# Starting the next chunk's ScalarE work before the current chunk's ladder on VectorE, in the input quantization of an adaLN block

## The chip, the cores and the metric

The kernel runs on one Trainium2 chip, on all 8 NeuronCores, each with one of the 8 batch elements. No data passes between the cores. The time is the device time in microseconds of the slowest core.

## What is computed

The reference is one adaLN layer on x of shape (8, 2048, 1024), with a gated recurrent mixer and a quantized feed-forward network. Cut to what matters here:

```python
def bitlinear(x, W, b):
    w_scale = clip(mean(abs(W)), EPS, None)
    Wq = clip(round(W / w_scale), -1, 1) * w_scale
    x_scale = clip(max(abs(x), axis=-1, keepdims=True), EPS, None)
    xq = clip(round(x * (127 / x_scale)), -128, 127) * (x_scale / 127)
    return einsum('bnd,hd->bnh', xq, Wq) + b

mod = silu(c) @ wmod            # six vectors: sa, ca, ga, sb, cb, gb
h = layernorm(x) * (1 + ca) + sa
x = x + ga * mixer(h)           # three 1024x1024 products, a scan over 2048 tokens
h = layernorm(x) * (1 + cb) + sb
x = x + gb * bitlinear(gelu(bitlinear(h, W1, b1)), W2, b2)   # hidden size 4096
```

The change touches the rounding of x in the first `bitlinear`: every element of h, times 127 over its token's maximum, is rounded to an integer.

## The kernel before, in words

A core holds its 2048 tokens along the free dimension and the 1024 features as KC = 8 chunks of 128 partitions. A chunk is a tile of 128x2048 in bf16. `X`, `Hh` and `X2` each hold eight chunks. The program is written engine by engine: `p.on(engine, function, wait, inc)` appends a function to the engine's list, with the semaphore counts that it waits for and the one that it increments. Order on an engine is the order of these calls. `sDV` counts VectorE's steps, `sAC` ScalarE's. Behind the functions stands the class `Ser` (line 85 on), which makes each VectorE, ScalarE and GpSimd instruction wait for the one before it on the same engine; nearly all rows therefore carry its line, L100 (the wait itself is L99). Where a function increments a counter, `ser_flush_wait` (L92) waits for the engine's last instruction first, and then the counter goes up; L56 is the increment behind it in `p.on`, L51 the one of a step without an instruction.

The stages in order: loads and statistics of the weights, the mixer (L734), the second layer norm with the scales of each token, the quantization of h, the first feed-forward product (L1066), the ternary form of W2, the second product (L1306, with the quantization of the hidden values in it), and its other three groups (L1346).

The quantization of h runs between `build_bcast`, which puts 127 over the token's maximum into `B127`, and `emit_tern`, which prepares the first weight slab. It goes over the eight chunks in `Hh`, in place. `xlad_u` multiplies the chunk by `B127` into `QUU` (VectorE). `xlad_act` takes the absolute value into `QY` and the sign into `QSG` (ScalarE). `xlad_dve` rounds on VectorE with a ladder: it adds 128, takes 127.5 off into `QRA`, and for the bits 64 down to 1 compares `QRA` with the bit into `QT` and subtracts; then it takes the integer part, puts the sign back and writes the chunk. `QUU`, `QAU`, `QY`, `QR0`, `QRA`, `QRB`, `QT`, `QNA` are eight 2048-wide parts of `X`, whose contents are no longer needed; `QSG` is `RB`. The names with R0, RB, NA and `QAU` are not used by the loop before; `MB` was the broadcast mean of the layer norm and is free by then. The first product waits for `xq_done`, the count after the last chunk.

The quantization of the hidden values in the second product (L1306's stage) has the same ladder on pairs of chunks of 128x4096, and there the multiply of the next pair is already placed inside the ladder of the current one (`emit_ulad`).

Of the kernel before, what the change touches and what calls it, by code (L numbers as in the profile page):

```python
# [8 lines left out]
AF = mybir.ActivationFunctionType  # L9
ALU = mybir.AluOpType  # L10
# [4 lines left out]
KC = D // 128  # L15
# [91 lines left out]
def build_nc():  # L107
    nc = bass.Bass("TRN2", target_bir_lowering=False)
    p = Prog()
# [43 lines left out]
    def sb(name, shape, dt):  # L153
        return nc.alloc_sbuf_tensor(name, shape, dt).ap()

    X = sb("X", [128, KC * L], BF16)
    Hh = sb("Hh", [128, KC * L], BF16)
# [3 lines left out]
    MB = sb("MB", [128, L], BF16)  # L161
# [5 lines left out]
    B127 = sb("B127", [128, L], BF16)  # L167
# [31 lines left out]
    QUU, QAU = XS(0, 2048), XS(2048, 4096)  # L199
    QY, QR0 = XS(4096, 6144), XS(6144, 8192)  # L200
    QRA, QRB = XS(8192, 10240), XS(10240, 12288)
    QT, QNA = XS(12288, 14336), XS(14336, 16384)
    QSG = RB[:, 0:2048]
# [43 lines left out]
    for s in semnames:  # L247
        p.sem(s)

    chunk = lambda t, k: t[:, k * L:(k + 1) * L]  # L250
# [4 lines left out]
         inc=("sCN", 16), dma=True)  # L255
    p.on("scalar", lambda E: E.dma_start(out=CPB[:], in_=cpack_b),
         inc=("sCN", 16), dma=True)
    p.on("scalar", lambda E: E.dma_start(out=IDNF[:], in_=idnf),
         inc=("sCN", 16), dma=True)
# [3 lines left out]
    for k in range(KC):  # L263
# [3 lines left out]
             wait=w, inc=(sx, 16))  # L267
        p.on("vector", lambda E, k=k: E.tensor_copy(chunk(X, k), xstg[k % 2]),
             wait=[(sx, p.cnt[sx])], inc=("sDV", 1))
# [3 lines left out]
         wait=[("sCN", cn_all)], inc=("sAC", 1))  # L273
# [143 lines left out]
    for t in range(48):  # L417
# [4 lines left out]
            inc=("sMD", 1) if t == 47 else None)  # L422
    mm_modc = p.cnt["sMD"]
    p.on("vector", lambda E: E.tensor_copy(MODC[:], PB[2][:, 0:48]),
         wait=[("sMD", mm_modc)], inc=("sDV", 1))
# [43 lines left out]
    def ws2_fin(E):  # L469
# [10 lines left out]
         wait=[("sDV", ws2_done)])  # L480
    p.on("tensor", lambda E: E.matmul(PB[7][:, 1:2], ONESRf[:],
                                      WSrow[0:1, 3:4], start=True, stop=True),
         inc=("sMM", 1))
# [11 lines left out]
    for k in range(KC):  # L495
        wv = [("sDV", modc_done)] if k == 0 else []
        for j in range(NNT):
# [3 lines left out]
                wait=wv if j == 0 else [],  # L501
                inc=("sM3", 1) if (k == KC - 1 and j == NNT - 1) else None)
# [17 lines left out]
    for k in range(KC):  # L520
        wv = [("sM3", st1_mm[k - 2])] if k >= 2 else []
        p.on("vector", lambda E, k=k: E.tensor_tensor(
            sq1[k % 2], chunk(X, k), chunk(X, k), ALU.mult),
            wait=wv, inc=("sDV", 1))
        sqdv = p.cnt["sDV"]
        for j in range(NNT):
# [4 lines left out]
                wait=[("sDV", sqdv)] if j == 0 else [],  # L531
                inc=("sM3", 1) if j == NNT - 1 else None)
# [28 lines left out]
    for j in range(NNT):  # L561
# [3 lines left out]
            wait=[("sAC", rstd1_ac)] if j == 0 else [],  # L565
            inc=("sM3", 1) if j == NNT - 1 else None)
# [10 lines left out]
    for j in range(NNT):  # L577
# [3 lines left out]
            wait=[("sAC", bc1e_ac)] if j == 0 else [],  # L581
            inc=("sM3", 1) if j == NNT - 1 else None)
# [12 lines left out]
    for k in range(KC):  # L595
        wv = [("sDV", bc1_done)] if k == 0 else [("sAC", p.cnt["sAC"])]

        def ln_apply_v(E, k=k, src=X):
# [6 lines left out]
            wait=[("sDV", p.cnt["sDV"])], inc=("sAC", 1))  # L605
# [79 lines left out]
    if DEBUG_TAPS:  # L685
        p.on("gpsimd", lambda E: E.dma_start(out=tap_hln, in_=Hh[:]),
             wait=[("sAC", p.cnt["sAC"])], inc=("sTAP", 16), dma=True)
        p.on("gpsimd", lambda E, v=p.cnt["sTAP"]: E.wait_ge(sems["sTAP"], v))
        p.on("gpsimd", lambda E: E.dma_start(out=tap_mod, in_=MODC[:]),
             inc=("sTAP", 16), dma=True)  # L690
# [179 lines left out]
    for k in range(KC):  # L870
        wv = [("sDV", bc2_done)] if k == 0 else []

        def h2_v(E, k=k):
# [6 lines left out]
            wait=[("sDV", p.cnt["sDV"])], inc=("sAC", 1))  # L880
        acn = p.cnt["sAC"]
        M1n = XS(4096, 6144)
        if k == 0:
# [3 lines left out]
                wait=[("sAC", acn)], inc=("sDV", 1))  # L887
        else:
# [3 lines left out]
                wait=[("sAC", acn)], inc=("sDV", 1))  # L892
# [4 lines left out]
        inc=("sDV", 1))  # L897
# [38 lines left out]
    def build_bcast(vec_tile, out_tile, after_dv):  # L936
        for g4 in range(4):
            pp = g4 % 2
            wv = [("sDV", after_dv)] if g4 == 0 else []
            if g4 >= 2:  # L940
                wv += [("sAC", p.cnt["sAC"])]
            for b4 in range(4):
                blk = g4 * 4 + b4
                p.on("vector", lambda E, blk=blk, b4=b4, v=vec_tile, pp=pp:
                     E.tensor_scalar(
                         WSB[:, (pp * 4 + b4) * 128:(pp * 4 + b4) * 128 + 128],
                         IDN[:], v[:, blk:blk + 1], None, ALU.mult),
                     wait=wv if b4 == 0 else [], inc=("sDV", 1))
                dvn = p.cnt["sDV"]
                p.on("tensor", lambda E, blk=blk, b4=b4, pp=pp: E.matmul(  # L950
                    PB[pp][:, b4 * 128:(b4 + 1) * 128], ONES128[:],
                    WSB[:, (pp * 4 + b4) * 128:(pp * 4 + b4) * 128 + 128],
                    start=True, stop=True),
                    wait=[("sDV", dvn)],
                    inc=("sMM", 1) if b4 == 3 else None)
            mmn = p.cnt["sMM"]
            p.on("scalar", lambda E, g4=g4, o=out_tile, pp=pp:
                 E.activation(o[:, g4 * 512:(g4 + 1) * 512],
                              PB[pp][:, 0:512], AF.Identity),
                 wait=[("sMM", mmn)], inc=("sAC", 1))  # L960
        p.on("vector", None, wait=[("sAC", p.cnt["sAC"])], inc=("sDV", 1))
        return p.cnt["sDV"]

    b127_done = build_bcast(VB127, B127, xs_done)
    bs1_done = build_bcast(VBS1, BS1, b127_done)

    def xlad_u(E, src_bf):
        return E.tensor_tensor(QUU, src_bf, B127[:], ALU.mult)

    def xlad_act(E):  # L970
        E.activation(QY, QUU, AF.Abs)
        return E.activation(QSG, QUU, AF.Sign)

    def xlad_dve(E, dst_bf):
        E.tensor_scalar(QY, QY, 128.0, None, ALU.add)
        E.tensor_scalar(QRA, QY, -127.5, None, ALU.add)
        for bit in (64.0, 32.0, 16.0, 8.0, 4.0, 2.0, 1.0):
            E.tensor_scalar(QT, QRA, bit, bit, ALU.is_ge, ALU.mult)
            E.tensor_tensor(QRA, QRA, QT, ALU.subtract)
        E.scalar_tensor_tensor(QT, QRA, -1.0, QY, ALU.mult, ALU.add)  # L980
        return E.scalar_tensor_tensor(dst_bf, QT, -127.5, QSG,
                                      ALU.add, ALU.mult)

    for k in range(KC):
        wv = [("sDV", bs1_done)] if k == 0 else []
        p.on("vector", lambda E, k=k: xlad_u(E, chunk(Hh, k)),
             wait=wv, inc=("sDV", 1))
        p.on("scalar", xlad_act, wait=[("sDV", p.cnt["sDV"])],
             inc=("sAC", 1))
        p.on("vector", lambda E, k=k: xlad_dve(E, chunk(Hh, k)),  # L990
             wait=[("sAC", p.cnt["sAC"])], inc=("sDV", 1))
    xq_done = p.cnt["sDV"]
    if DEBUG_TAPS:
        p.on("gpsimd", lambda E: E.dma_start(out=tap_xq, in_=Hh[:]),
             wait=[("sDV", p.cnt["sDV"])], inc=("sTAP", 16), dma=True)
        def tapstm(E):
# [4 lines left out]
             inc=("sTAP", 16), dma=True)  # L1001
        p.on("gpsimd", lambda E, v=p.cnt["sTAP"]: E.wait_ge(sems["sTAP"], v))
        p.on("gpsimd", lambda E: E.dma_start(out=tap_bs[:, L:2 * L], in_=BS1[:]),
             inc=("sTAP", 16), dma=True)
# [46 lines left out]
    for hc in range(HC):  # L1051
        if hc + 2 < HC:
            emit_tern(hc + 2)
        for j in range(NNT):
            jp = (hc * NNT + j) % 4
            gidx = hc * NNT + j
            for k in range(KC):
                wv = []
                if k == 0:
                    wv = [tern_dvs[hc]]  # L1060
                    if gidx == 0:
                        wv += [("sDV", xq_done)]
                    if gidx >= 4:
# [6 lines left out]
                     wait=wv, inc=("sMM", 1) if k == KC - 1 else None)  # L1070
# [5 lines left out]
                wait=[("sMM", mmn)], inc=("sDV", 1))  # L1076
# [6 lines left out]
                wait=[("sDV", dvn)], inc=("sAC", 1))  # L1083
        gelu_acs.append(p.cnt["sAC"])
        H1T = H1Tp[hc % 2]
        if hc == 0:
# [3 lines left out]
                 wait=[("sAC", gelu_acs[-1])], inc=("sDV", 1))  # L1090
        else:
# [3 lines left out]
                 wait=[("sAC", gelu_acs[-1])], inc=("sDV", 1))  # L1095
# [3 lines left out]
             wait=[("sAC", gelu_acs[-1])], inc=(ssp, 16), dma=True)  # L1099
        spill_sps.append((ssp, p.cnt[ssp]))  # L1100
        if DEBUG_TAPS and hc == 0:
            p.on("gpsimd", lambda E: E.dma_start(out=tap_h1, in_=H1Tp[0]),
                 inc=("sTAP", 16), dma=True)
# [9 lines left out]
        inc=("sDV", 1))  # L1113
# [6 lines left out]
    for u in range(2 * KC):  # L1120
        s, h = u // 2, u % 2
        st = u % 4
        if u < 4:
            wv = [("sSPa", p.cnt["sSPa"]), ("sSPb", p.cnt["sSPb"])]
        else:
            wv = [("sDV", w2u_dv[u - 4])]
# [3 lines left out]
            wait=wv, inc=(sw, 16))  # L1130
# [17 lines left out]
        if h == 1:  # L1148
# [5 lines left out]
                                                     k=HC)),  # L1154
                wait=[("sDV", w2u_dv[u])], inc=(ssp_s, 16), dma=True)
# [14 lines left out]
    if DEBUG_TAPS:  # L1170
        p.on("gpsimd", lambda E: E.dma_start(out=tap_bs[:, 2 * L:3 * L],
                                             in_=BS2[:]),
             wait=[("sDV", bs2_done)], inc=("sTAP", 16), dma=True)
# [3 lines left out]
             inc=("sTAP", 16), dma=True)  # L1177
# [31 lines left out]
    for gi, (d0, d1) in enumerate([(0, 1), (2, 3), (4, 5), (6, 7)]):  # L1209
        if gi == 0:  # L1210
# [45 lines left out]
            for pr in range(NPAIR):  # L1256
                pf = pr % 2
                if pr + 1 < NPAIR:
# [17 lines left out]
                     wait=[("sAC", uacts[pr])], inc=("sDV", 1))  # L1276
# [3 lines left out]
                def dve_tail(E, pf=pf):  # L1280
# [15 lines left out]
                    wait=[("sDV", lad_vals[(0, pr)])], inc=(sh1, 16),  # L1296
# [3 lines left out]
                for kch in range(2):  # L1300
                    for nt in range(NNT):
                        for di, d in enumerate((d0, d1)):
# [11 lines left out]
                                 wait=mmw  # L1314
                                 if (kch == 0 and nt == 0 and di == 0)
                                 else [],
                                 inc=("sMM", 1)
# [3 lines left out]
        else:  # L1321
            for kc in range(HC):
                pp = kc % 4
                srd = ["sRDa", "sRDb", "sW1a", "sW1b"][pp]
                wv = []
                if kc < 4:
                    wv = [("sMM", last_mm)]
# [3 lines left out]
                elif (gi, kc - 4) in mm_vals:  # L1331
                    wv = [("sMM", mm_vals[(gi, kc - 4)])]
# [9 lines left out]
                for nt in range(NNT):  # L1342
                    for di, d in enumerate((d0, d1)):
# [6 lines left out]
                             wait=mmw if (nt == 0 and di == 0) else [],  # L1350
                             inc=("sMM", 1) if (nt == NNT - 1 and di == 1)
# [5 lines left out]
        for ei in range(8):  # L1357
# [4 lines left out]
            wv = [("sMM", mm_g)] if ei == 0 else []  # L1362
            if ei >= 2 or gi >= 1:
# [4 lines left out]
                wait=wv, inc=("sDV", 1))  # L1368
            dvn = p.cnt["sDV"]
            if ei == 7:  # L1370
# [4 lines left out]
                wait=[("sDV", dvn)], inc=("sAC", 1))  # L1375
# [4 lines left out]
                wait=[("sAC", acn)], inc=("sDV", 1))  # L1380
# [3 lines left out]
                wait=[("sDV", dvn2)], inc=(sfin, 16), dma=True)  # L1384
# [114 lines left out]
```

How the kernel before makes its waits and increments, by code:

```python
    def on(self, eng, fn, wait=(), inc=None, dma=False):  # L40
        sems = self.sems
        serialized = (eng in ("vector", "scalar", "gpsimd")) and not dma
        for (s, v) in wait:
            if v > 0:
                self.ops[eng].append(lambda E, s=s, v=v: E.wait_ge(sems[s], v))
        if inc is not None:
            sname, amt = inc
            val = self.inc(sname, amt)
            if fn is None:
                self.ops[eng].append(
                    lambda E, s=sname, a=amt: E.sem_inc(sems[s], a))
            elif serialized:
                def run(E, f=fn, s=sname, a=amt):
                    f(E)
                    E.ser_flush_wait()
                    E.sem_inc(sems[s], a)
                self.ops[eng].append(run)
            else:
                self.ops[eng].append(
                    lambda E, f=fn, s=sname, a=amt: f(E).then_inc(sems[s], a))
            return val
        assert fn is not None
        self.ops[eng].append(fn)
        return None
# [1 line left out]
    def barrier(self):  # L66
        for e in ENGINES:
            self.inc("sBR", 1)
        target = self.cnt["sBR"]
        sems = self.sems
        for e in ENGINES:
            self.ops[e].append(lambda E: E.sem_inc(sems["sBR"], 1))
            self.ops[e].append(lambda E: E.wait_ge(sems["sBR"], target))
# [16 lines left out]
    def ser_flush_wait(self):  # L90
        if self._n:
            self._e.wait_ge(self._s, self._n)
```

## Time and profile before

| | |
|---|---|
| median of 3 runs | 2732.17 us (2727.35 to 2735.86) |
| the profiled execution | 2734.15 us |
| its span on the slowest core, core 3 | 2732.5 us (the cores: 2712.9 to 2732.5) |
| TensorE busy | 934.0 us, 34% of the span |
| VectorE busy | 1430.3 us, 52% |
| ScalarE busy | 580.3 us, 21% |
| GpSimd busy | 191.9 us, 7% |
| mean granted TensorE clock | 0.676 on core 3 |

The profile is of one execution. The span goes from a core's first to its last instruction; the small rest of the execution's time lies outside it. In the rows below DVE is VectorE, ACT is ScalarE, POOL is GpSimd, SP is SyncE, PE the matmuls and PEld the weight loads of TensorE. A bracket at the end of a row gives how long the engine was idle before it and what released it; a q behind an engine's name is its sequencer, which waits and increments. PEclk is TensorE's granted clock as a share of full speed.

### The profile page before, as it was taken

What the parts mean: (1) busy time and instruction counts of PE and PEld (TensorE: products, weight loads), DVE (VectorE), ACT (ScalarE), POOL (GpSimd) and SP (SyncE); (2) the same over time, 40 slices, a digit from 0 to 9 for tenths busy, and PEclk for the clock granted to TensorE, in tenths of its full rate; (3) what the DMA queues carried; (4) which work ended last, traced back from release to release, by engine and by line L of the source; (5) the groups of instructions that cost most, each with busy time, mean ns of one, the idle gap of its engine ahead of it and who ended that gap; (6) DMA issues with size and microseconds to landing.
All of it is one profiled execution on the core that took longest, in us unless ns stands there. A gap on an engine that the chain in (4) does not pass through costs nothing.

```text
span 2732.5 us, 14949 instructions; the slowest of 8 cores (2712.9 to 2732.5 us)
## 1 busy us (share of the span) xinstructions
PE 934.0 (34%) x3428; PEld 338.2 (12%) x3428; DVE 1430.3 (52%) x1188; ACT 580.3 (21%) x476; POOL 191.9 (7%) x180
## 2 busy tenths in 40 slices
PE   1772324453551210005877601010110111154744
PEld 0110001121220000002333200000000000021211
DVE  1010042435345457777666664899999999701011
ACT  0202322524515311112222200212112112000000
POOL 0000000010100000002222210000000000000000
PEclk9885566776765655557898955555555555587978
DMA  6864301010000000002322193111211211176965
GB/s 224 296 205 154 108 0 46 23 46 14 33 23 30 1 0 0 0 0 78 108 108 106 65 293 122 38 54 62 77 54 62 77 53 62 73 249 206 307 233 193
DMA packets 71847, 265.46 MB, mean 97 GB/s; under 512 B 7632, under 2 KB 8016, under 8 KB 64336
## 3 DMA queue, kind: packets, MB, share of 16 engines
q1 hardware_dynamic: 36896, 155.20, 16.7%
q0 software_dynamic: 18304, 67.12, 6.8%
q10 hardware_dynamic: 16560, 42.19, 4.8%
q8 instruction: 29, 0.48, 0.1%
q14 instruction: 58, 0.48, 0.1%
HBM read 214.15 MB, written 50.33 MB: 97 GB/s over the span
## 4 chain that ended last, share of the span: by engine, by line
DVE 47%; DMA 18%; PE 12%; ACT 11%; issue 8%; DVEq 2%; POOL 1%; ACTq 1%; SPq 0%; POOLq 0%
DVE X L100 20%; DVE Hh L100 12%; DVE SC L100 8%; PE PB L734 6%; DMA RB<-w2qsp 5%; DMA SC<-w2T 3%; ACT SC L100 3%; ACT X L100 3%; PE PB L1346 3%; DVE M L100 2%; DMA WSTG<-w2T 2%; DMA out_img<-SC 2%; ACT RB L100 2%; ACT WSB L100 2%; DMA SC<-xT 2%
## 5 line engine op out<-in xcount | busy, mean ns | idle before, releaser
L734 PE MATMUL PB<-Hh,WSB 128*128 128x512 bf16 x768 | 191.9, 417 | 245.0 <-POOLq L56 133.2
L100 DVE TENSOR_TENSOR SC<-PB,BS 128x512 f32<-128x512 f32 x160 | 110.7, 692 | 314.0 <-PE PB L1346 239.6
L100 DVE TENSOR_TENSOR X<-X 128x2048 bf16<-128x2048 bf16 (+1 forms) x120 | 206.8, 1723 | 14.9 <-PE PB L527 1.7
L1066 PE MATMUL PB<-Hh,W1Q 128*128 128x512 bf16 x512 | 124.4, 406 | 255.3 <-POOLq L56 223.4
L100 DVE TENSOR_SCALAR X<-X 128x2048 bf16<-128x2048 bf16 (+1 forms) x145 | 139.0, 959 | 54.6 <-ACTq L56 35.7
L100 ACT ACTIVATE X<-X 128x4096 bf16<-128x4096 bf16 (+1 forms) x24 | 73.2, 3049 | 420.0 <-DVEq L56 419.3
L1306 PE MATMUL PB<-Hh,M 128*128 128x512 bf16 x128 | 46.9, 547 | 307.6 <-DVEq L56 307.6
L1306 PE MATMUL PB<-X,RB 128*128 128x512 bf16 x128 | 45.7, 535 | 279.8 <-DVEq L56 279.8
L100 ACT ACTIVATE X<-SC,CPF 128x512 bf16<-128x512 f32 x128 | 92.5, 723 | 215.6 <-DVEq L56 213.4
L1346 PE MATMUL PB<-X,M 128*128 128x512 bf16 x384 | 96.1, 398 | 112.4 <-DMA M<-w2qsp 108.9
L1066 PE MATMUL PB<-Hh,RB 128*128 128x512 bf16 x512 | 122.4, 401 | 32.4 <-DVEq L56 32.4
L100 DVE TENSOR_TENSOR Hh<-Hh 128x4096 bf16<-128x4096 bf16 x56 | 128.4, 2293 | 5.8
L734 PEld LDWEIGHTS PB<-Hh,WSB 128*128 128x128 bf16 x768 | 80.2, 105 | 357.1 <-issue 283.1
L100 ACT ACTIVATE Hh<-Hh 128x4096 bf16<-128x4096 bf16 x16 | 57.9, 3617 | 247.6 <-DVEq L56 246.9
L100 ACT ACTIVATE SC<-SC,B2G,GBt 128x512 f32<-128x512 f32 x32 | 26.1, 814 | 384.7 <-DVEq L56 384.7
L1346 PE MATMUL PB<-X,RB 128*128 128x512 bf16 x384 | 90.1, 378 | 27.7 <-DMA RB<-w2qsp 26.2
L100 DVE TENSOR_SCALAR Hh<-Hh 128x4096 bf16<-128x4096 bf16 x72 | 88.3, 1227 | 18.3 <-ACTq L56 7.8
L1066 PEld LDWEIGHTS PB<-Hh,W1Q 128*128 128x128 bf16 x512 | 51.7, 103 | 327.7 <-issue 277.6
L100 DVE SCALAR_TENSOR_TENSOR X<-X 128x4096 bf16<-128x4096 bf16 (+1 forms) x24 | 89.1, 3714 | 2.5
L100 POOL TENSOR_TENSOR W1Q<-SC 128x1024 bf16<-128x1024 f32 x16 | 37.5, 2344 | 508.4 <-DVEq L56 500.3
L100 DVE TENSOR_REDUCE WSrow<-PB 1x1 f32<-1x512 f32 x3 | 2.0, 678 | 135.5 <-PE PB L354 135.1
L100 DVE SCALAR_TENSOR_TENSOR Hh<-Hh 128x4096 bf16<-128x4096 bf16 x16 | 70.8, 4425 | 1.7
(170 smaller groups left out, 1510.9 us busy)
## 6 DMA issues: line engine op xcount, KB each, us to landing
X<-h1qsp SPq DMA_DIRECT2D x96, 512.0 KB, 6.2
SC<-w1T POOLq DMA_DIRECT2D x32, 512.0 KB, 6.9
WSTG<-w1T SPq DMA_DIRECT2D x32, 512.0 KB, 3.3
h1sp<-X POOLq DMA_DIRECT2D x32, 512.0 KB, 3.1
WSTG<-wmodT SPq DMA_DIRECT2D x6, 2048.0 KB, 10.2
SC<-wmodT SPq DMA_DIRECT2D x12, 1024.0 KB, 9.4
SC<-w2T SPq DMA_DIRECT2D x12, 1024.0 KB, 8.0
M<-w2qsp ACTq DMA_DIRECT2D x48, 256.0 KB, 7.0
```

The costliest lines, as they stand in the source:

```text
L100: ins = f(*a, **k)
L734: E.matmul(PB[pp + gi][:, :], WSB[:, gi * 1024 + k * 128: gi * 1024 + (k + 1) * 128], ntile(Hh, k, j), start=(k == 0), stop=(k == KC - 1)),
L1066: E.matmul(PB[jp][:, :], w1q[hc % 4][:, k * 128:(k + 1) * 128], ntile(Hh, k, j), start=(k == 0), stop=(k == KC - 1)),
L1306: E.matmul(PB[4 * di + nt][:, :], W2R[2 * pf + kch][:, d * 128:(d + 1) * 128], FIN[pf][:, kch * 2048 + nt * 512: kch * 2048 + (nt + 1) * 512],
L1346: E.matmul(PB[4 * di + nt][:, :], W2R[pp][:, d * 128:(d + 1) * 128], H1Q2[pp][:, nt * 512:(nt + 1) * 512], start=(kc == 0), stop=(kc == HC ...
```

## The change

The loop over the eight chunks is reordered, and a second set of tiles is added. `x_u(k)` issues the multiply of chunk k on VectorE and its two activations on ScalarE. It is called for chunk 0 ahead of the loop, and in pass k for chunk k+1 before the ladder of chunk k. Even chunks use the tiles used so far, odd chunks use `QAU`, `QR0`, `QRB`, `QNA` and `MB`. The ladder of chunk k waits for the count of ScalarE noted for that chunk in `xact`. The instructions themselves, their shapes and their number stay as they were.

```diff
-    def xlad_u(E, src_bf):
-        return E.tensor_tensor(QUU, src_bf, B127[:], ALU.mult)
-
-    def xlad_act(E):
-        E.activation(QY, QUU, AF.Abs)
-        return E.activation(QSG, QUU, AF.Sign)
-
-    def xlad_dve(E, dst_bf):
-        E.tensor_scalar(QY, QY, 128.0, None, ALU.add)
-        E.tensor_scalar(QRA, QY, -127.5, None, ALU.add)
-        for bit in (64.0, 32.0, 16.0, 8.0, 4.0, 2.0, 1.0):
-            E.tensor_scalar(QT, QRA, bit, bit, ALU.is_ge, ALU.mult)
-            E.tensor_tensor(QRA, QRA, QT, ALU.subtract)
-        E.scalar_tensor_tensor(QT, QRA, -1.0, QY, ALU.mult, ALU.add)
-        return E.scalar_tensor_tensor(dst_bf, QT, -127.5, QSG,
-                                      ALU.add, ALU.mult)
-
+    QSET = [(QUU, QY, QRA, QT, QSG), (QAU, QR0, QRB, QNA, MB[:])]
+    xact = {}
+
+    def x_u(k):
+        U, Y, RA, T, SG = QSET[k % 2]
+        p.on("vector", lambda E, k=k, U=U: E.tensor_tensor(
+            U, chunk(Hh, k), B127[:], ALU.mult),
+            wait=([("sDV", bs1_done)] if k == 0 else []), inc=("sDV", 1))
+        p.on("scalar", lambda E, U=U, Y=Y, SG=SG: (
+            E.activation(Y, U, AF.Abs),
+            E.activation(SG, U, AF.Sign))[-1],
+            wait=[("sDV", p.cnt["sDV"])], inc=("sAC", 1))
+        xact[k] = p.cnt["sAC"]
+
+    x_u(0)
     for k in range(KC):
-        wv = [("sDV", bs1_done)] if k == 0 else []
-        p.on("vector", lambda E, k=k: xlad_u(E, chunk(Hh, k)),
-             wait=wv, inc=("sDV", 1))
-        p.on("scalar", xlad_act, wait=[("sDV", p.cnt["sDV"])],
-             inc=("sAC", 1))
-        p.on("vector", lambda E, k=k: xlad_dve(E, chunk(Hh, k)),
-             wait=[("sAC", p.cnt["sAC"])], inc=("sDV", 1))
+        if k + 1 < KC:
+            x_u(k + 1)
+        U, Y, RA, T, SG = QSET[k % 2]
+
+        def xdve(E, k=k, Y=Y, RA=RA, T=T, SG=SG):
+            E.tensor_scalar(Y, Y, 128.0, None, ALU.add)
+            E.tensor_scalar(RA, Y, -127.5, None, ALU.add)
+            for bit in (64.0, 32.0, 16.0, 8.0, 4.0, 2.0, 1.0):
+                E.tensor_scalar(T, RA, bit, bit, ALU.is_ge, ALU.mult)
+                E.tensor_tensor(RA, RA, T, ALU.subtract)
+            E.scalar_tensor_tensor(T, RA, -1.0, Y, ALU.mult, ALU.add)
+            return E.scalar_tensor_tensor(chunk(Hh, k), T, -127.5, SG,
+                                          ALU.add, ALU.mult)
+        p.on("vector", xdve, wait=[("sAC", xact[k])], inc=("sDV", 1))
     xq_done = p.cnt["sDV"]
```

## Rows read from the trace of the kernel before

**Rows 1.** The page: busy time, share of the span and instructions of each engine.

```profile
PE 934.0 (34%) x3428; PEld 338.2 (12%) x3428; DVE 1430.3 (52%) x1188; ACT 580.3 (21%) x476; POOL 191.9 (7%) x180
```

**Rows 2.** Busy time by stage on core 3; "x" counts instructions.

```profile
core 3: us, PE busy (x) PEld busy (x) DVE busy (x) ACT busy (x) POOL busy (x), PEclk, DMA share, GB/s
1027.90:1245.30 217.40, 0.00 (x0) 0.00 (x0) 165.05 (x152) 30.57 (x16) 0.00 (x0) 0.50 0.00 0
1245.30:1566.00 320.70, 246.81 (x1024) 102.99 (x1024) 215.43 (x254) 93.79 (x129) 92.76 (x63) 0.92 0.27 97
...
2390.00:2732.50 342.50, 185.35 (x768) 70.61 (x768) 39.43 (x57) 23.50 (x29) 15.68 (x29) 0.83 0.72 238
```

**Rows 3.** Timeline of one chunk: start us, duration us, instruction.

```profile
1082.18 1.22 DVE L100 TENSOR_TENSOR X<-Hh,B 128x2048 bf16<-128x2048 bf16 x1 [0.26 <-DVE Hh L100]
1083.66 1.91 ACT L100 ACTIVATE X<-X 128x2048 bf16<-128x2048 bf16 x1 [23.20 <-DVEq L56]
1085.66 1.91 ACT L100 ACTIVATE RB<-X 128x2048 bf16<-128x2048 bf16 x1
1087.83 2.29 DVE L100 TENSOR_SCALAR X<-X 128x2048 bf16<-128x2048 bf16 x3 [4.43 <-ACTq L56]
1090.23 1.23 DVE L100 TENSOR_TENSOR X<-X 128x2048 bf16<-128x2048 bf16 x1
...
1106.73 2.29 DVE L100 SCALAR_TENSOR_TENSOR Hh<-X,RB 128x2048 bf16<-128x2048 bf16 x1
1109.29 1.22 DVE L100 TENSOR_TENSOR X<-Hh,B 128x2048 bf16<-128x2048 bf16 x1 [0.27 <-DVE Hh L100]
```

**Rows 4.** VectorE's waits, 1027.9 to 1245.3: total us, times, longest.

```profile
DVE X L100 <- ACTq L56: 35.7, 8, 4.7
DVE X L100 <- DVE Hh L100: 1.9, 7, 0.3
```

**Rows 5.** Instructions by form, 1027 to 1245: busy us, mean ns, idle before.

```profile
L100 DVE TENSOR_TENSOR X<-X 128x2048 bf16<-128x2048 bf16 x56 | 68.6, 1225 | 5.8
L100 DVE TENSOR_SCALAR X<-X 128x2048 bf16<-128x2048 bf16 x72 | 50.0, 694 | 42.9 <-ACTq L56 35.7 <-DVE X L100 0.5
L100 DVE SCALAR_TENSOR_TENSOR X<-X 128x2048 bf16<-128x2048 bf16 x8 | 18.3, 2292 | 0.8
L100 DVE SCALAR_TENSOR_TENSOR Hh<-X,RB 128x2048 bf16<-128x2048 bf16 x8 | 18.3, 2292 | 0.8
L100 ACT ACTIVATE X<-X 128x2048 bf16<-128x2048 bf16 x8 | 15.3, 1910 | 164.9 <-DVEq L56 164.9
L100 ACT ACTIVATE RB<-X 128x2048 bf16<-128x2048 bf16 x8 | 15.3, 1910 | 0.7
L100 DVE TENSOR_TENSOR X<-Hh,B 128x2048 bf16<-128x2048 bf16 x8 | 9.8, 1225 | 3.5 <-DVE Hh L100 1.9 <-DVEq L51 1.7
```

**Rows 6.** Timelines of ScalarE and VectorE in the stage after 1697 us.

```profile
1706.86 7.33 ACT L100 ACTIVATE Hh<-Hh 128x4096 bf16<-128x4096 bf16 x2 [10.06 <-DVEq L56]
...
1878.86 3.89 DVE L100 TENSOR_SCALAR Hh<-Hh 128x4096 bf16<-128x4096 bf16 x3 [0.34 <-DVE X L100]
...
1893.30 2.55 DVE L100 TENSOR_TENSOR X<-X,B 128x2048 bf16<-128x2048 bf16 x2 [0.69 <-DVE Hh L100]
1896.11 7.33 ACT L100 ACTIVATE X<-X 128x4096 bf16<-128x4096 bf16 x2 [34.13 <-DVEq L56]
1896.12 1.23 DVE L100 TENSOR_SCALAR Hh<-Hh 128x4096 bf16<-128x4096 bf16 x1 [0.27 <-DVE X L100]
1897.45 2.29 DVE L100 TENSOR_TENSOR Hh<-Hh 128x4096 bf16<-128x4096 bf16 x1
...
1907.31 1.23 DVE L100 TENSOR_SCALAR Hh<-Hh 128x4096 bf16<-128x4096 bf16 x1
1908.64 2.29 DVE L100 TENSOR_TENSOR Hh<-Hh 128x4096 bf16<-128x4096 bf16 x1
```

**Rows 7.** Timelines around the end of the last ladder, and SyncE's before.

```profile
881.41 1.75 SPq L1024 DMA_DIRECT2D WSTG<-w1T  x4
...
1242.92 2.29 DVE L100 SCALAR_TENSOR_TENSOR Hh<-X,RB 128x2048 bf16<-128x2048 bf16 x1
1245.55 0.75 DVE L100 TENSOR_SCALAR SC<-WSTG,WS1i 128x1024 f32<-128x1024 f32 x1 [0.34 <-DVE Hh L100]
...
1250.16 16.21 PE L1066 MATMUL PB<-Hh,W1Q 128*128 128x512 bf16 x64 [223.38 <-POOLq L56]
```

**Rows 8.** L1066 on core 0, then core 7: duration min/median/max, first and last start.

```profile
L1066 PE MATMUL PB<-Hh,W1Q x512: 376/379/631, 1242.2 to 1536.6; 128*128 128x512 bf16 x171
L1066 PE MATMUL PB<-Hh,RB x512: 376/379/634, 1259.0 to 1553.3; 128*128 128x512 bf16 x171
...
L1066 PE MATMUL PB<-Hh,W1Q x512: 376/379/634, 1235.8 to 1528.4; 128*128 128x512 bf16 x171
L1066 PE MATMUL PB<-Hh,RB x512: 376/379/634, 1252.2 to 1546.5; 128*128 128x512 bf16 x171
```

**Rows 9.** Timeline of TensorE, 1276 to 1300 (the last row is cut at 1300).

```profile
1276.50 7.07 PE L1066 MATMUL PB<-Hh,RB 128*128 128x512 bf16 x32 [2.84 <-DVEq L56]
1286.41 7.07 PE L1066 MATMUL PB<-Hh,W1Q 128*128 128x512 bf16 x32 [2.84 <-DVEq L56]
1296.67 3.57 PE L1066 MATMUL PB<-Hh,W1Q 128*128 128x512 bf16 x8 [3.19 <-DVEq L56]
```

## The prediction

> **What bounds the kernel now.** I read three views before the diff. First the page's busy times: VectorE is busy for 52% of the span, ScalarE for 21%, TensorE for 34% [rows 1]. That is an average, so the second view is the table of stages [rows 2]. The reader should look there for the stage the change touches, 1027.9 to 1245.3 us on the slowest core. It lasts 217.4 us; TensorE, GpSimd and DMA do nothing in it, VectorE is busy for 165.05 us and ScalarE for 30.57 us. The third view is the order of time inside one chunk of this stage [rows 3]. It shows a strict handover: VectorE multiplies (1.22 us), ScalarE runs two activations of 1.91 us, and VectorE starts its ladder 4.43 us after its own multiply ended. Each engine idles while the other works. The list of waits confirms it: VectorE waited for ScalarE 8 times, 35.7 us in total [rows 4]. Nothing else was waited for longer than 1.9 us in total, so this stage is a chain of VectorE and ScalarE, and every us taken from the chain ends the stage a us earlier.
>
> **The parts of a chunk.** Grouped by form [rows 5], the stage holds per chunk one multiply Hh by B127 (1.225 us), two activations (1.910 us each), nine TENSOR_SCALAR (0.694), seven TENSOR_TENSOR (1.225) and two SCALAR_TENSOR_TENSOR (2.292). The ladder's 18 instructions make 9 x 0.694 + 7 x 1.225 + 2 x 2.292 = 19.4 us; their 17 gaps are about 0.105 us each, from starts 1087.83 and 1106.73 [rows 3]: the ladder runs from 1087.83 to 1106.73 + 2.29 = 1109.02, which is L = 21.19 us. From the ladder's end to the next multiply it is 0.27 us. So one chunk takes 0.27 + 1.22 + 4.43 + 21.19 = 27.11 us, and the starts of the ladder in 1087.83 and of the multiplies at 1082.18 and 1109.29 agree (27.11 apart) [rows 3].
>
> **What the change does to the chain.** The instructions are the same in number, form and size: 8 multiplies, 16 activations, 8 ladders. No DMA moves, no queue but VectorE's and ScalarE's is touched. Only VectorE's order is new: u0, u1, ladder 0, u2, ladder 1, ..., u7, ladder 6, ladder 7, with a second set of tiles so that ScalarE can work on chunk k+1 while the ladder of chunk k runs.
>
> Before the first ladder nothing is gained: ScalarE gets u0 as before, and ladder 0 starts 4.43 us after u0 ends. u1 fits inside that wait (0.27 + 1.22 = 1.49 us of 4.43), so it costs nothing; if the cover were gone it would cost 1.49 us.
>
> From then on the activations of chunk k+1 start when u(k+1) ends, and need about 4.4 us, while VectorE has a 21.19 us ladder in front of it. They are done some 17 us before they are wanted, so the wait is met when VectorE comes to it. Between ladders 0 to 5 and their successors stand: a gap, u, a gap. The first gap I take at 0.27 as now [rows 3]. For the second, a ladder whose activations are long done, the trace has its like in the stage after 1697 us, which has exactly this order already: 0.34 us when the ladder's head begins [rows 6]. That is 0.27 + 1.22 + 0.34 = 1.83 us, six times 11.0 us. Ladder 7 follows ladder 6 with 0.34 us. Together 11.3 us.
>
> Now the same pieces before: seven times 0.27 + 1.22 + 4.43 = 5.92 us, 41.4 us. The rest is common to both (4.43 + 8 x L). **The sum: 41.4 - 11.3 = 30.1 us less.** Seven of the eight waits of 4.43 us go, and one multiply goes under the wait that is left; what is paid back are seven gaps.
>
> **What could take it back: the engines side by side.** Before, VectorE and ScalarE never worked together in this stage; after, 14 activations (26.7 us) lie under ladder instructions. The nearest rows are again of the late stage, where two activations of 128x4096 run from 1896.11 to 1903.44 [rows 6]. VectorE's TENSOR_SCALAR took 1.23 us and its TENSOR_TENSOR 2.29 us under them, and 1.23 and 2.29 at 1907.31 and 1908.64 without them; the pair of activations took 7.33 us with VectorE busy, and 7.33 us at 1706.86 before the first ladder of that stage, when VectorE had nothing to do. So I cost overlap at nothing. Bounds for the gaps: from above, the multiply of the late stage once began 0.69 us after the instruction before it [rows 6]; six gaps of that size instead of 0.27 take back 2.5 us (27.6 us gained). From below, no gap is shorter than the 0.10 between two ladder instructions; thirteen gaps of 0.10 in place of six of 0.27 and seven of 0.34 give 2.7 us more (32.8 us gained). I take the middle rows, since they have the same order of instructions and semaphores.
>
> The page "VectorE: DVE Perf Modes" of the Trainium skill, section "The DRAIN you can't avoid", says that a semaphore after each VectorE instruction adds nothing to a run of them. By it all gaps would be alike and the gain would be the 32.8 us of the lower bound, 2699.4 us instead of 2702. The trace differs from it: 0.27 and 0.34 us stand where an instruction follows a flush and an increment, 0.10 where it does not [rows 3, 6], and I follow the trace.
>
> **Is the gain handed on?** The next work is VectorE's too: the ternary split of the first weight slab begins 0.34 us after the last ladder, GpSimd subtracts, TensorE starts at 1250.16 [rows 7]. Its weights were requested by SyncE from 881.41 us on, 360 us ahead, so no load is late when the stage moves up by 30 us [rows 7]. RB, which the first tile set still uses for signs, and MB, now used by the second, are next written by GpSimd and VectorE after all ladders, as before. The stage that follows has a pace of its own: on cores 0 and 7, with different starts, its first to last matmul start takes 1553.3 - 1242.2 = 311.1 and 1546.5 - 1235.8 = 310.7 us [rows 8]. It is shifted, not changed. All eight cores have the same stage of ladders, so all shift together, and the load on HBM at the end, where DMA is busy for 72% [rows 2], finds the cores as far apart as now.
>
> **The sum against the time.** The profiled execution took 2734.15 us with a span of 2732.5 on core 3, so 1.65 us lie outside the span. 2734.15 - 30.1 = 2704.0. That execution is 2.0 us above the median of the runs, 2732.17. The forecast for the median is 2732.17 - 30.1 = 2702.1 us, ratio 0.989. Three runs before spread from 2727.35 to 2735.86; I hold 0.3% (8 us) to be about what a measurement tells from no change.
>
> **Rivals.**
> *Overlap costs what it hides.* If ladder instructions stood still while ScalarE reads and writes the same memory, the gain would be 30.1 - 26.7 = 3.4 us, 2728.8 us, no change that can be told. For it: no row shows a 128x2048 form of these two side by side. Against it: the late stage's equal durations with and without ScalarE [rows 6]. 2 in 100.
> *The wait stays.* If ScalarE's wait count or a shared tile still made it run after the ladder, all would stand as now, 2732 us. The counts are taken right behind each multiply, and the two sets share no tile. 1 in 100.
> *TensorE's clock in the next stage.* This one ends slower. TensorE is idle through the ladders at a granted clock of 0.50, its 1.2 GHz level [rows 2], and after them runs at a mean of 0.92. A group of 32 matmuls at 2.4 GHz takes 7.07 us inside a period of 9.9 us that VectorE sets [rows 9]: TensorE has 2.84 us in hand. At the low level 8 matmuls took 3.57 us [rows 9], 14.3 us for 32, and a group would take 4.4 us more than the period. If the earlier start left the clock low, seven whole groups at the low level would eat the gain, and all 31 would make it 135 us, so 2732 + 105 = 2837 us. Against it: the idle stretch before TensorE's start is 223.4 us now [rows 7] and only some 193 us after, both cold starts, and on both cores read the stage has the same length [rows 8]. 1 in 100.
> The page "TensorE: Matmul & The Clock Gate" of the Trainium skill, section "A second HAM failure mode: psum-queue depth-cycling", says that small pauses between groups of matmuls can make the clock swing between its levels and cost throughput. By that rule the length of this stage could change with the pauses, which the change leaves as they are. The mean of 0.92 agrees that it swings, and no row shows it costing the stage anything.
>
> **How the numbers follow.** My forecast, the chain shortened by 27.6 to 32.8 us and handed on, has 96 in 100. Its centre is 2702.1; the two bounds give 2699.4 to 2704.6, and the spread of the runs adds 4.8 us below and 3.7 above: 2694.6 to 2708.3. I give 2694 to 2709, which leaves some 1.5 in 10 outside with the rivals. Chances: faster 0.96, same 0.03, slower 0.01.
>
> **What the profile after would show.** VectorE's wait for ScalarE in the stage once at about 4.4 us, in total under 7 us; the stage 187 us long instead of 217; a period of 23.0 us a chunk; both activations of a chunk inside the ladder's first third; durations 0.69, 1.22, 2.29 and 1.91 unchanged; about 311 us for the next stage. The forecast is wrong if ladder instructions under an activation are longer, if a new wait appears where ladder 7 or the first split begins, or if a later stage grows by what this one lost.

## The result, and the profile after

The changed kernel takes 2703.84 us (median of 9 runs, 2697.21 to 2709.24), the kernel before 2734.6 us in the same comparison (10 runs, 2727.35 to 2742.23). The ratio is 0.9888, with a 95% interval from 0.9874 to 0.9903: 30.8 us less, 1.1% faster. Forecast were 2702 us and a ratio of 0.989.

The busy times of VectorE, ScalarE and GpSimd stay as they were to half a us [rows 1], as they must when only an order changes; TensorE's is 7 us lower, on another core of another execution:

```profile
PE 926.8 (34%) x3428; PEld 336.5 (12%) x3428; DVE 1430.0 (53%) x1188; ACT 579.9 (21%) x476; POOL 192.2 (7%) x180
```

The table of stages on the slowest core, which is core 7 in this execution, shows where the time went. The first row is the stage of the change, the second the first product [rows 2].

```profile
core 7: us, PE busy (x) PEld busy (x) DVE busy (x) ACT busy (x) POOL busy (x), PEclk, DMA share, GB/s
1027.90:1215.20 187.30, 0.00 (x0) 0.00 (x0) 165.09 (x153) 30.57 (x16) 0.00 (x0) 0.50 0.00 0
1215.20:1536.00 320.80, 240.95 (x1024) 101.61 (x1024) 215.65 (x255) 93.68 (x129) 92.77 (x63) 0.94 0.27 97
```

VectorE is busy for 165 us as before, in 187.3 us instead of 217.4. The timeline of VectorE shows the idle times around the multiplies; the chunks left out repeat the pattern [rows 3]:

```profile
1027.99 1.23 DVE L100 TENSOR_TENSOR X<-Hh,B 128x2048 bf16<-128x2048 bf16 x1 [1.69 <-DVEq L51]
1029.48 1.22 DVE L100 TENSOR_TENSOR X<-Hh,B 128x2048 bf16<-128x2048 bf16 x1 [0.26 <-DVE X L100]
1033.64 2.29 DVE L100 TENSOR_SCALAR X<-X 128x2048 bf16<-128x2048 bf16 x3 [2.94 <-ACTq L56]
1055.10 1.22 DVE L100 TENSOR_TENSOR X<-Hh,B 128x2048 bf16<-128x2048 bf16 x1 [0.26 <-DVE Hh L100]
1056.66 2.29 DVE L100 TENSOR_SCALAR X<-X 128x2048 bf16<-128x2048 bf16 x3 [0.34 <-DVE X L100]
1078.12 1.23 DVE L100 TENSOR_TENSOR X<-Hh,B 128x2048 bf16<-128x2048 bf16 x1 [0.27 <-DVE Hh L100]
...
1149.10 2.29 DVE L100 TENSOR_SCALAR X<-X 128x2048 bf16<-128x2048 bf16 x3 [0.71 <-DVE X L100]
...
1193.64 2.29 DVE L100 TENSOR_SCALAR X<-X 128x2048 bf16<-128x2048 bf16 x3 [0.34 <-DVE Hh L100]
1215.17 0.75 DVE L100 TENSOR_SCALAR SC<-WSTG,WS1i 128x1024 f32<-128x1024 f32 x1 [0.34 <-DVE Hh L100]
```

Two multiplies stand at the head, and one wait for ScalarE is left, of 2.94 us. With the second multiply and its gap inside (0.26 + 1.22) it is 4.42 us, as before. From the multiply at 1055.10 to the one at 1078.12 it is 23.02 us a chunk, where it was 27.11. From the first multiply to the first ternary split the stage runs from 1027.99 to 1215.17, 187.18 us. Before, on core 3, it ran from this multiply to the split at 1245.55 [rows 7], 217.60 us:

```profile
1027.95 1.23 DVE L100 TENSOR_TENSOR X<-Hh,B 128x2048 bf16<-128x2048 bf16 x1 [1.69 <-DVEq L51]
```

That is 30.42 us less. The length on all eight cores of each execution is 217.57 to 217.61 before and 187.16 to 187.20 after.

The list of waits of the stage [rows 4], total us, times, longest:

```profile
DVE X L100 <- ACTq L56: 2.9, 1, 2.9
DVE X L100 <- DVE X L100: 2.6, 7, 0.7
DVE X L100 <- DVE Hh L100: 1.9, 7, 0.3
```

The activations of a chunk now end 3.8 us after the next ladder has begun, so they lie beside its first instructions, TENSOR_SCALAR and TENSOR_TENSOR:

```profile
1056.58 1.91 ACT L100 ACTIVATE X<-X 128x2048 bf16<-128x2048 bf16 x1 [19.02 <-DVEq L56]
1056.66 2.29 DVE L100 TENSOR_SCALAR X<-X 128x2048 bf16<-128x2048 bf16 x3 [0.34 <-DVE X L100]
1058.59 1.91 ACT L100 ACTIVATE RB<-X 128x2048 bf16<-128x2048 bf16 x1
```

These forms keep their means, and so do the activations [rows 5]:

```profile
L100 DVE TENSOR_TENSOR X<-X 128x2048 bf16<-128x2048 bf16 x56 | 68.6, 1225 | 5.8
L100 DVE TENSOR_SCALAR X<-X 128x2048 bf16<-128x2048 bf16 x72 | 50.0, 694 | 12.5 <-ACTq L56 2.9 <-DVE X L100 2.4 <-DVE Hh L100 0.3
L100 DVE SCALAR_TENSOR_TENSOR X<-X 128x2048 bf16<-128x2048 bf16 x8 | 18.3, 2292 | 0.8
L100 ACT ACTIVATE X<-X 128x2048 bf16<-128x2048 bf16 x8 | 15.3, 1911 | 117.1 <-DVEq L56 116.8 <-ACT RB L100 0.3
```

TensorE's matmuls of the first product on core 7 (the line is now 1071) take 1530.5 - 1219.8 = 310.7 us from first to last start, the same 310.7 as before [rows 8]:

```profile
L1071 PE MATMUL PB<-Hh,W1Q x512: 376/379/634, 1219.8 to 1512.5; 128*128 128x512 bf16 x171
L1071 PE MATMUL PB<-Hh,RB x512: 376/379/634, 1236.2 to 1530.5; 128*128 128x512 bf16 x171
```

### The profile page after: what moved, and what is told of

Its sections match the earlier page's. It is cut to its first block, busy times and chain, and to the rows that moved or that the text cites. A ratio compares the mean times of both kernels' runs of the same rounds, so it can differ in the third digit from the quotient of the medians.

```text
span 2698.5 us, 14949 instructions; the slowest of 8 cores (2676.3 to 2698.5 us)
## 1 busy us (share of the span) xinstructions
PE 926.8 (34%) x3428; PEld 336.5 (12%) x3428; DVE 1430.0 (53%) x1188; ACT 579.9 (21%) x476; POOL 192.2 (7%) x180
## 4 chain that ended last, share of the span: by engine, by line
DVE 49%; DMA 18%; PE 12%; ACT 11%; issue 8%; DVEq 2%; ACTq 1%; POOL 1%; SPq 0%; POOLq 0%
DVE X L100 20%; DVE Hh L100 12%; DVE SC L100 9%; PE PB L734 6%; DMA RB<-w2qsp 6%; DMA SC<-w2T 4%; ACT SC L100 3%; PE PB L1351 3%; ACT X L100 2%; DVE M L100 2%; DMA SC<-xT 2%; DMA out_img<-SC 2%; ACT WSB L100 2%; DMA WSTG<-w2T 2%; ACT Hh L100 2%
## 5 line engine op out<-in xcount | busy, mean ns | idle before, releaser
L306 PE MATMUL PB<-WSTG,SCf 128*1 128x512 f32 x96 | 47.6, 653 | 65.9 <-DMA WSTG<-wmodT 65.2
```

What stands on the lines that cost most here:

```text
L306: p.on("tensor", lambda E, j=j, k=k: E.matmul(PB[j % 2][0:1, :], SCf[:, k:k + 1], mod_piece(j, k), start=(k == 0), stop=(k == KC - 1)), wa ...
```

## The experiments

The edits below are against the changed kernel, except where the kernel before is named.

**The second set of tiles alone.** Both sets are used in turn, but each multiply stands right ahead of its own ladder.

```diff
-    x_u(0)
     for k in range(KC):
-        if k + 1 < KC:
-            x_u(k + 1)
+        x_u(k)
```

> The second set of tiles alone, in the order of the kernel before: each multiply stands right ahead of its own ladder. My theory (the order takes the waits away): nothing changes, about 2734 us, VectorE's eight waits of 4.43 us all still there, the stage at 217 us. Rival (a conflict between tiles was part of the wait, and the second set frees it): some us below 2734, with waits shorter than 4.43.

Measured: 2736.48 us beside 2735.61 for the kernel before, ratio 0.9994 (0.9969 to 1.0019). The stage is 217.57 us long on its slowest core, and the waits are those of before:

```profile
DVE X L100 <- ACTq L56: 35.7, 8, 4.7
```

The tiles gain nothing by themselves. They make the new order possible; the order brings the gain.

**The new order within pairs only.**

```diff
-        if k + 1 < KC:
-            x_u(k + 1)
+        if k % 2 == 0:
+            x_u(k)
+            x_u(k + 1)
```

with the first `x_u(0)` taken out.

> The new order only within pairs of chunks: u0, u1, ladder 0, ladder 1, u2, u3, ladder 2, ladder 3 and so on. My theory counts the handovers left: a pair costs 1.22 + 4.43 + L + 0.34 + L + 0.27, which is 5.58 us less than two chunks before, four times 22.3 us less than the kernel before: about 2712 us. VectorE's waits: four of 2.9 us (4.43 less the second multiply), none between the two ladders of a pair. Rival (overlap costs something per activation under a ladder): four pairs under a ladder cost a little, and the result lies above 2712 by a share that grows with seven overlapped chunks in the full change.

Measured: 2714.07 us, ratio 0.9916 (0.9886 to 0.9945), 21.5 us less than before. The stage takes 194.94 us on the slowest core, 22.66 less than the 217.60 of before. Its timeline shows the pattern of a pair: the wait of 2.94 us ahead of the first ladder, 0.33 us between the two ladders, and again two multiplies.

```profile
1041.15 2.29 DVE L100 TENSOR_SCALAR X<-X 128x2048 bf16<-128x2048 bf16 x3 [2.94 <-ACTq L56]
1062.69 2.29 DVE L100 TENSOR_SCALAR X<-X 128x2048 bf16<-128x2048 bf16 x3 [0.33 <-DVE Hh L100]
1084.14 1.22 DVE L100 TENSOR_TENSOR X<-Hh,B 128x2048 bf16<-128x2048 bf16 x1 [0.26 <-DVE Hh L100]
1085.63 1.22 DVE L100 TENSOR_TENSOR X<-Hh,B 128x2048 bf16<-128x2048 bf16 x1 [0.26 <-DVE X L100]
1089.79 0.69 DVE L100 TENSOR_SCALAR X<-X 128x2048 bf16<-128x2048 bf16 x1 [2.94 <-ACTq L56]
```

The gain goes with the number of handovers left on the chain.

**ScalarE's work doubled, in both orders.** Both activations of a chunk are issued twice, once in the changed kernel (below) and once in the kernel before (the same in `xlad_act`).

```diff
             E.activation(Y, U, AF.Abs),
-            E.activation(SG, U, AF.Sign))[-1],
+            E.activation(SG, U, AF.Sign),
+            E.activation(Y, U, AF.Abs),
+            E.activation(SG, U, AF.Sign))[-1],
```

> The changed kernel with both activations of each chunk issued twice (same inputs and outputs), so ScalarE needs 7.9 us a chunk instead of 3.9. My theory: only chunk 0 shows it, 2 x 2.0 = 4.0 us more than the changed kernel, about 2708 us; ladder instructions stay at 0.69, 1.22 and 2.29 us under the longer overlap. Rival (ScalarE beside VectorE slows it): each of seven ladders grows by the same share for twice the overlap; at a tenth of the overlapped time that is 2.7 us more, at all of it 27 us.

> The kernel before with both activations of each chunk issued twice. My theory: all eight chunks show it, 8 x 2 x 2.0 = 32 us more, about 2766 us, VectorE's waits at 8.4 us each. With the run above it gives the worth of the cover: 58 us between the two orders instead of 30. Rival (part of the wait of 4.43 us is a fixed cost of the handover that grows with nothing): the same here, so this run alone does not tell them apart; the wait less the two activations (4.43 - 3.9 = 0.5 us) must stay the same if it is.

Measured: new order 2713.11 us, ratio 0.9912 (0.9883 to 0.9941); old order 2764.51 us, ratio 1.01 (1.0065 to 1.0135). The lengths of the stage are sharper than the totals: 191.13 us on the slowest core in the new order, 3.95 more than the 187.18 of the changed kernel (forecast 4.0); 249.30 us in the old order, 31.7 more than before (forecast 32). Between the orders lie 58.2 us. The new order's total is 5 us above the expected 2708, which is still inside its interval (2704 to 2719 us); the stage itself shows nothing of them, so what they are is open. VectorE's waits, new order and then old order:

```profile
DVE X L100 <- ACTq L56: 6.9, 1, 6.9
```

```profile
DVE X L100 <- ACTq L56: 67.4, 8, 8.4
```

8.4 less four activations with their small gaps (7.9) leaves the same half us for the two handovers as 4.43 less 3.9. The ladder's TENSOR_TENSORs in the new order, whose first ones are now beside ScalarE for 7.9 us a chunk:

```profile
L100 DVE TENSOR_TENSOR X<-X 128x2048 bf16<-128x2048 bf16 x56 | 68.6, 1225 | 5.8
```

Twice the overlap costs the TENSOR_TENSORs not a nanosecond of their mean. The SCALAR_TENSOR_TENSORs stand at the ladder's end, behind the activations even here; the next pair of runs is the test of them. The rival that overlap costs what it hides is out: by it the stage would have grown by some 27 us more here, and it grew by the 4 us of chunk 0 alone.

**A short ladder, in both orders.** `Y` holds 128 plus the value in bf16, and between 128 and 256 a bf16 number is an integer. The value is rounded as soon as 128 is added; the 16 instructions between that one and the last only split bits that are already whole. (Worked out in bf16, they even leave the result half a step off, since `T` becomes `Y` less 0.5, which bf16 does not hold above 128.) This was worked out, not measured; it lets the ladder shrink to two instructions (shown in the changed kernel; the kernel before gets the same last step in `xlad_dve`):

```diff
             E.tensor_scalar(Y, Y, 128.0, None, ALU.add)
-            E.tensor_scalar(RA, Y, -127.5, None, ALU.add)
-            for bit in (64.0, 32.0, 16.0, 8.0, 4.0, 2.0, 1.0):
-                E.tensor_scalar(T, RA, bit, bit, ALU.is_ge, ALU.mult)
-                E.tensor_tensor(RA, RA, T, ALU.subtract)
-            E.scalar_tensor_tensor(T, RA, -1.0, Y, ALU.mult, ALU.add)
-            return E.scalar_tensor_tensor(chunk(Hh, k), T, -127.5, SG,
+            return E.scalar_tensor_tensor(chunk(Hh, k), Y, -128.0, SG,
                                           ALU.add, ALU.mult)
```

> The kernel before with a short ladder in the quantization of h: behind the addition of 128, whose bf16 result is already 128 plus the rounded value, one instruction takes 128 off and puts the sign on. Two VectorE instructions (0.69 + 0.10 + 2.29 = 3.09 us) stand in place of 18 (21.19 us). All waits for ScalarE stay at 4.43 us. Expected: 8 x 18.1 = 145 us less than the kernel before, about 2590 us, a chunk every 9.0 us.

> The changed kernel with the same short ladder. The cover is now thin: between the end of one multiply and the moment VectorE wants its activations stand 0.34 + 3.09 + 0.27 + 1.22 = 4.9 us, and ScalarE needs 4.43 us. My theory: still just covered, the same 30 us between the two orders as with the long ladder, about 2560 us, a chunk every 4.9 us. Rival (overlap costs): ScalarE is at work for 78% of the stage, so any slowing of either engine breaks the cover, waits come back and the distance to the old order with a short ladder falls below 30 us. Rival (TensorE's clock): its idle stretch ahead of the first product shrinks from 193 us to some 50 us; if that mattered, the first product's length would move from 311 us.

Measured: old order 2589.0 us, ratio 0.9463 (0.9437 to 0.949); new order 2562.31 us, ratio 0.9366 (0.9339 to 0.9393). The stage takes 72.41 and 42.67 us on the slowest cores. Their distance is 29.7 us, where it was 30.4 with the long ladder. The totals are 26.7 us apart, which their intervals (7 us to each side) do not tell from 30. The timeline of the new order's end shows the 0.7 us:

```profile
1069.13 1.91 ACT L100 ACTIVATE X<-X 128x2048 bf16<-128x2048 bf16 x1 [1.01 <-DVEq L56]
1069.21 0.69 DVE L100 TENSOR_SCALAR X<-X 128x2048 bf16<-128x2048 bf16 x1 [0.34 <-DVE X L100]
1070.01 2.29 DVE L100 SCALAR_TENSOR_TENSOR Hh<-X,RB 128x2048 bf16<-128x2048 bf16 x1
1071.13 1.91 ACT L100 ACTIVATE MB<-X 128x2048 bf16<-128x2048 bf16 x1
1073.30 0.69 DVE L100 TENSOR_SCALAR X<-X 128x2048 bf16<-128x2048 bf16 x1 [1.00 <-ACTq L56]
```

Ahead of the last ladder stands no multiply any more, so the cover there is only ladder 6 with its gap, some 3.4 us against 4.43, and VectorE waits 1.00 us instead of 0.34. Everywhere else 4.9 us still cover 4.43. The rule of the prediction holds at its edge, in the one place where the cover is short: what is missing (1.0 us) comes back us for us.

In this run the last step does lie beside activations, and its mean is what it was without them (a group over the stage):

```profile
L100 DVE SCALAR_TENSOR_TENSOR Hh<-X,MB 128x2048 bf16<-128x2048 bf16 x4 | 9.2, 2293 | 0.4
```

This pair also speaks on the clock. In the new order TensorE starts the first product after 48.45 us of idle time instead of 193. On six cores the granted clock over 315 us with the product is 0.90 to 0.94; on cores 4 and 5 it is 0.79 and 0.81. Here is the row of core 5, and its matmuls in the answer by line:

```profile
core 5: us, PE busy (x) PEld busy (x) DVE busy (x) ACT busy (x) POOL busy (x), PEclk, DMA share, GB/s
1061.00:1376.00 315.00, 274.41 (x1024) 108.97 (x1024) 211.70 (x252) 92.65 (x128) 90.47 (x63) 0.81 0.28 99
```

```profile
L1066 PE MATMUL PB<-Hh,W1Q x512: 379/437/631, 1061.4 to 1355.7; 128*128 128x512 bf16 x171
L1066 PE MATMUL PB<-Hh,RB x512: 421/437/438, 1079.1 to 1374.1; 128*128 128x512 bf16 x171
```

The median matmul is 437 ns instead of 379, and the product takes 312.7 us instead of 310.7. A slower TensorE costs this stage only 2 us. A group of 32 matmuls now takes 8.56 us instead of 7.07 [rows 9], but most groups still begin 9.9 us after the one before, and TensorE still waits for VectorE ahead of them:

```profile
1118.06 8.56 PE L1066 MATMUL PB<-Hh,RB 128*128 128x512 bf16 x32 [1.35 <-DVEq L56]
```

**The short ladder in the second product too**, where the same 18 instructions work on 128x4096:

```diff
                 # ... the head of the ladder, ahead of the next pair's multiply, is taken out
                 def dve_tail(E, pf=pf):
                     # ... the rest of the ladder is taken out
+                    E.tensor_scalar(FIN[pf], FIN[pf], 128.0, None, ALU.add)
+                    return E.scalar_tensor_tensor(FIN[pf], FIN[pf], -128.0,
                                                   FSG[pf], ALU.add, ALU.mult)
+                p.on("vector", dve_tail, wait=[("sAC", uacts[pr])],
+                     inc=("sDV", 1))
```

> As the run above, and the ladder of the second product's first group is short too: its 18 instructions on 128x4096 become two. VectorE needs some 9 us a pair of chunks there instead of 41.1. Expected: VectorE is no longer what sets the pace; ScalarE's 7.3 us, and the chain spill, load, multiply, activations, last step become it, some 16 us a pair, 400 us less than the run above: about 2160 us.

Measured: 2218.17 us, ratio 0.8106 (0.8081 to 0.8131), 58 us above the expected 2160. I had expected some 16 us a pair; two pairs take 41.5 us, from the multiply at 1557.48 to the one at 1598.93, or 20.7 us each, and VectorE now waits for loads:

```profile
DVE Hh L100 <- DMA M<-w2qsp: 93.8, 8, 13.2
DVE X L100 <- DMA RB<-w2qsp: 87.5, 8, 13.1
```

Here the multiply of the next pair stands ahead of the last steps of this one, and waits for its loads. They go into tiles that the pair before it has just left, and in the source they wait until its result is spilled from there:

```profile
1560.29 7.33 ACT L100 ACTIVATE Hh<-Hh 128x4096 bf16<-128x4096 bf16 x2 [13.77 <-DVEq L56]
1566.77 0.72 POOL L1271 DMA_DIRECT2D h1qsp<-X  x1 [20.46 <-DVEq L56]
1572.09 0.37 SPq L1228 DMA_DIRECT2D X<-h1sp  x1
1578.40 2.56 DVE L100 TENSOR_TENSOR X<-X,B 128x2048 bf16<-128x2048 bf16 x2 [12.28 <-DMA RB<-w2qsp]
1581.30 1.23 DVE L100 TENSOR_SCALAR Hh<-Hh 128x4096 bf16<-128x4096 bf16 x1 [0.34 <-DVE X L100]
```

Spill and load fill the 12.28 us in which VectorE is idle, while the activations that its next step needs were done at 1567.62. The order that pays off in front of a long ladder puts a DMA wait in front of a short one. That the other order would win this time back was not run by itself.

**The fastest version**: no ScalarE in either quantization. The edit is on the kernel before, in whose loop it takes the place of the three functions.

```diff
+    def x_round(E, k):
+        E.tensor_tensor(QUU, chunk(Hh, k), B127[:], ALU.mult)
+        return E.tensor_scalar(chunk(Hh, k), QUU, 12582912.0, -12582912.0,
+                               ALU.add, ALU.add)
```

and the same two steps on a pair in the second product, behind its load; there the multiply is no longer placed ahead.

> No ScalarE in either quantization: a multiply by B127, then one VectorE instruction that adds 1.5 x 2^23 and takes it off again, which rounds to an integer if VectorE computes in fp32 and rounds after each operation. A chunk takes 1.22 + 0.69 + gaps = 2.3 us, the stage some 19 us instead of 187; in the second product VectorE needs 3.9 us a pair, and the pace is that of the spill and load of 1 MB each, 12 to 14 us a pair. About 2090 us. If VectorE rounds only at the end of the instruction, the values are not rounded to integers; the time is the same.

Measured: 2017.09 us, ratio 0.7375 (0.7348 to 0.7401). The stage takes 18.4 us, from the first multiply at 1021.66 to the split at 1040.06:

```profile
1021.66 1.22 DVE L100 TENSOR_TENSOR X<-Hh,B 128x2048 bf16<-128x2048 bf16 x1 [1.69 <-DVEq L51]
1023.00 0.69 DVE L100 TENSOR_SCALAR Hh<-X 128x2048 bf16<-128x2048 bf16 x1
...
1040.06 0.75 DVE L100 TENSOR_SCALAR SC<-WSTG,WS1i 128x1024 f32<-128x1024 f32 x1 [0.34 <-DVE Hh L100]
```

The total is 73 us below the expected 2090. A pair in the second product takes 10.7 us (the multiplies at 1520.01 and 1647.90 are twelve pairs apart), not 12 to 14; over sixteen pairs that is 21 to 53 us of the 73, and where the rest lies was not traced. With this version the wait that this study is about has no place left: one VectorE instruction of 0.69 us stands where two activations, their handovers and 18 instructions stood. Whether VectorE rounds to an integer between the two additions, on which the values of this version rest, no run here was made to tell; the version with the short ladders does not need it.

## Why the prediction was right

**The chain.** The stage was a chain of VectorE and ScalarE with nothing beside it, and each us taken from it arrived at the end. The pairs (22.66 us for a forecast 22.3), the doubled activations (3.95 and 31.7 for 4.0 and 32) and the tiles alone (nothing) show it from three sides.

**The sum.** Forecast were 30.1 us, measured are 30.42 in the stage. The 0.3 us are single delays outside the pattern, which the sum left out. Before, one wait for ScalarE was 4.7 instead of 4.43 us and one gap inside a ladder 0.5 instead of 0.10 [rows 4, 5]; after, one gap is 0.71 instead of 0.34. Together about 0.67 us before and 0.37 after. What makes these delays was not tried.

**The gaps.** The sizes taken, 0.27 and 0.34 us, were the right ones: 0.26 or 0.27 ahead of each multiply, 0.34 ahead of a ladder whose activations are done. Their source was less alike than I said. The late stage does not have "exactly this order": its multiply stands inside a ladder, and its 0.34 us stand behind the last step of a ladder, while here they stand behind a multiply. The gap came out the same behind either, which the rows of before could not show. The rule of the Trainium skill ("VectorE: DVE Perf Modes", section "The DRAIN you can't avoid"), that a semaphore after each instruction adds nothing to a run of copies, does not carry over to this step: where the flush wait and the counter's increment stand between two instructions, the gap is 0.16 us and more above the 0.10 inside a ladder, in every chunk. By that rule the gain would have been 32.8 us; the stage shows 30.42.

**Overlap at nothing.** TENSOR_TENSOR and TENSOR_SCALAR keep their means of 1225 and 694 ns with the activations beside the ladder's head, and TENSOR_TENSOR with twice the overlap too; the activations take 1911 ns after 1910. For SCALAR_TENSOR_TENSOR only the short ladder shows it, 2293 ns after 2292.

**The hand-on.** The first product kept its 310.7 us. The rest of the kernel moved up with it: the totals differ by 30.8 us (interval 26.5 to 34.5) where the stage differs by 30.4. That these two agree to 0.4 us is luck; the equal lengths of the next stage are the stronger sign.

**The signs I had named.** One of them needs a better reading: I said that the one wait left would show as about 4.4 us. It shows as 2.94, since the second multiply now stands inside it. A wait in the list is idle time, not the time from request to release.

**The clock.** The rival that ends slower did not come: over the first product the granted clock was 0.94 after 193 us of idle time, and 0.92 before, and the short ladder shows what a lower clock cost where one did appear: 2 us at 0.81. A first product held at the 1.2 GHz level throughout did not occur in any run, so my price for that case stays untried.

## What to carry to other kernels

Where two engines hand work to and fro and both are idle in turns, count the handovers on the chain, and price each by the idle time in the timeline less the gap that stays (4.43 less 0.34 here, 28.6 us for seven; the other 1.5 us of the 30.1 is the multiply that moves into the first wait). One chunk of lead and a second set of tiles take all of them away but the first, as long as the work put in front of a wait is longer than the other engine's turn. Then ask what the long engine's work is for: the reorder brought 30 us, and dropping instructions that round a value already rounded brought 145 us in the same stage.

## What the runs showed that I had not expected

**A level between the two clocks.** In the run with the short ladder and the new order, cores 4 and 5 held a granted clock of 0.79 to 0.81 over the first product, while cores 6 and 7 of the same die had 0.90 to 0.93. It is a level and not a mean of two: in slices of 20 us from 1085 to 1365, core 5 reads 0.81 in every one. The same came in the run with both ladders short, this time on cores 0 and 1: 0.82 on each from 1070 to 1370 us, and 0.94 and 0.93 on cores 2 and 3. The first product's granted clock stayed between 0.92 and 0.95 on all cores of every other profiled run, over 255 to 265 us of the product. The Trainium skill ("TensorE: Matmul & The Clock Gate", section "Seeing it yourself") tells of a current limit that takes a whole die to 13/16 of the clock, 0.81. The level agrees; that it takes all cores of the die does not, in these two traces. What brings it on in some executions is open; a short idle time ahead of the product does not do it by itself, for in the fastest version TensorE idles only 24 us there and no core reads below 0.93.

**A stage more exact than the kernel.** The stage has the same length on the eight cores of an execution to 0.05 us, before and after, while the cores of one execution end up to 22 us apart (2676.3 to 2698.5 us after). The start of the stage differs between cores by as much: 1006.7 to 1028.0 us. What the change does to this stage, in which DMA does nothing, can be read in one profile to a tenth of a us; the totals spread over 12 us in nine runs after and 15 us in ten before.
